# Opening of a vision transformer kernel by channel, the bias on TensorE, and the rounding of w1 in six halves

## What is computed

```python
y = einsum('bchw,rc->bhwr', x, W_repr) + b_repr        # 5 representations of 3 channels
h = patches of y (16 x 16) projected by W_proj (5, 192, 256), summed over the 5, + b_proj
h = h + attention(layernorm(h), W_qkv, W_out)          # 12 heads of 64, 36 tokens per image
z = layernorm(h)
expert = argmax(softmax(z @ gate_w + gate_b))          # 8 experts
h = h + (gelu(z @ w1[e] + b1[e]) @ w2[e] + b2[e])      # e is each token's expert
```

## Time and profile before

| | |
|---|---|
| time, median of 3 executions | 329.94 us (329.91 to 331.65) |
| the profiled execution's own time | 332.25 us |
| its span, first to last instruction | 330.5 us |
| mean granted clock of TensorE, share of full speed | 0.918 |
| busy: TensorE products | 280.2 us (85%) |
| busy: VectorE | 205.5 us (62%) |
| busy: ScalarE | 161.1 us (49%) |
| busy: GpSimd | 61.5 us (19%) |

### The profile page before, as it was taken

The page is one execution under the profiler, slowest core; times in us unless marked ns, Lnnn a source line. Parts: engine busy times, 40 slices in busy tenths (PEclk is TensorE's granted clock), DMA queues, the critical chain, the costliest instruction groups (busy, mean ns, idle before and its releaser), DMA issues.

```text
span 330.5 us, 6850 instructions
## 1 busy us (share of the span) xinstructions
PE 280.2 (85%) x2070; PEld 243.9 (74%) x2071; DVE 205.5 (62%) x585; ACT 161.1 (49%) x585; POOL 61.5 (19%) x105
## 2 busy tenths in 40 slices
PE   1677998899988899988899998957578999999982
PEld 1666887688967688967688876837467999988971
DVE  2986768835878836878825888144325565556530
ACT  3323488942579843578933479312014433442420
POOL 2711000103000103000103000020410443443231
PEclk9996999969999979999969999695959999999998
DMA  6889400000500000400000108756220122212100
GB/s 226 240 325 419 176 3 0 2 0 2 163 0 0 0 0 18 142 0 0 0 0 8 47 2 344 324 193 245 59 60 0 48 69 56 70 42 50 39 0 0
DMA packets 5727, 27.87 MB, mean 84 GB/s; under 512 B 1575, under 2 KB 2867, under 8 KB 5070
## 3 DMA queue, kind: packets, MB, share of 16 engines
q1 hardware_dynamic: 3630, 17.32, 15.0%
q10 hardware_dynamic: 288, 6.29, 4.6%
q0 software_dynamic: 1792, 4.04, 4.4%
HBM read 24.99 MB, written 3.34 MB: 86 GB/s over the span
## 4 chain that ended last, share of the span: by engine, by line
PE 61%; DVE 13%; ACT 11%; issue 8%; DMA 3%; POOL 1%; DVEq 1%; SPq 0%; POOLq 0%; ACTq 0%
PE psum L417 20%; PE psum L642 10%; PE psum L475 7%; ACT late L731 5%; PE psum L402 4%; PE psum L466 3%; PE psum L512 3%; PE psum L630 3%; PE psum L445 3%; PE psum L454 2%; DMA late<-w_proj 2%; DVE top L885 2%; DVE late L880 2%; DVE late L894 1%; DVE w1B L906 1%
## 5 line engine op out<-in xcount | busy, mean ns | idle before, releaser
L731 ACT ACTIVATE late<-late,top 108x108 f32<-108x108 f32 (+1 forms) x144 | 52.4, 373 | 3.3 <-DVE top L886 3.2
L417 PE MATMUL psum<-xn_hi,wq_parts 128*128 128x288 f32 x144 | 37.6, 329 | 2.4 <-DVE xnB_lo L862 1.4
L1186 POOL TENSOR_SCALAR veps<-mv 96x1 f32<-96x1 f32 x24 | 5.5, 229 | 180.9 <-DVE mv L844 180.5
L642 PE MATMUL psum<-w2s,kT 128*128 x192 | 34.7, 331 | 2.1 <-DVE kT L1113 1.3
L642 PEld LDWEIGHTS psum<-w2s,kT 128*128 128x128 f32 x192 | 30.8, 190 | 4.3 <-issue 4.2
L475 PE MATMUL psum<-wo,oT 128*96 128x192 f32 x144 | 31.0, 373 | 0.8 <-ACT oT L760 0.8
L417 PEld LDWEIGHTS psum<-xn_hi,wq_parts 128*128 128x128 f32 x144 | 25.9, 200 | 5.0 <-DVE rows L1004 1.7
L731 ACT ACTIVATION_READ_ACCUMULATOR late<-late,top 108x1 f32 (+1 forms) x144 | 28.4, 197 | 0.0
L475 PEld LDWEIGHTS psum<-wo,oT 128*96 128x96 f32 x144 | 26.1, 190 | 3.0 <-issue 1.4
L402 PE MATMUL psum<-late,xb 128*96 128x192 f32 x144 | 25.8, 331 | 2.9 <-issue 2.9
L454 PE MATMUL psum<-ident,late 108*108 108x108 f32 (+1 forms) x144 | 20.5, 270 | 8.7 <-DVE late L894 8.0
(11 more groups left out here) (157 smaller groups left out, 627.4 us busy)
## 6 DMA issues: line engine op xcount, KB each, us to landing
w2s<-w SPq DMA_DIRECT2D x1, 4608.0 KB, 15.0
xb<-xT SPq DMA_DIRECT2D x4, 864.0 KB, 6.9
w1A_in<-w ACTq DMA_DIRECT2D x1, 3072.0 KB, 10.2
w1B_in<-w ACTq DMA_DIRECT2D x1, 3072.0 KB, 18.7
late<-b SPq DMA_DIRECT2D x2, 1536.0 KB, 7.1
token_table<-rows SPq DMA_DIRECT2D x4, 432.0 KB, 3.4
late<-w_proj SPq DMA_DIRECT2D x1, 960.0 KB, 5.5
kT<-b SPq DMA_DIRECT2D x1, 768.0 KB, 11.4
```

Of the source, the lines that this page charges most:

```text
L417: mm = pe.matmul(dst, lhsT, rhs, start=(i == 0), stop=(i == len(parts) - 1))
L642: mm = pe.matmul(psum[:, 6, 0:D], hidT[i % 2][:, c * P:(c + 1) * P], w2s[:, bass.ds(e, 1), c, :], start=(c == 0), stop=(c == FCH - 1))
L731: ex = act.activation(head, head, ACT.Exp, bias=top[0:n, u % 3, i:i + 1], scale=LOGIT_SCALE, accum_out=total[0:n, u % 3, i:i + 1])
```

## The change

1. `w_repr` and `b_repr` come as one array, written out for 128 partitions by the host, in one load instead of two; `wr` and `br` are views of it.
2. The bias: `wb` and its five VectorE operations are gone. TensorE multiplies the projection itself with b_repr, a column of `br` repeated 96 times as the stationary operand, in ten products, and b_proj in an eleventh. ScalarE, not VectorE, copies the bias out of PSUM, between its two pairs of casts of w_qkv. The bias comes ahead of token tile 0.
3. The 32 transposes wait for the identity alone, not for w_proj.
4. `weff` is summed channel by channel with a semaphore for each. TensorE multiplies all three token tiles with channel 0, then channel 2 (GpSimd's), then channel 1, in three PSUM banks.
5. `split_wq` is parted in two. The second part for the first columns moves behind the three normalisations.
6. w1 is rounded in six casts of 1024 columns at steps 5 to 10 (for w1A two, for w1B's first half two, for its second two) instead of three of 2048 at steps 1, 3 and 5. VectorE's four subtractions stand at steps 6, 7 and 8 and behind the value copy (group 1, first half) at the seam, instead of steps 2, 3, 6 and 7.

```diff
-W1_ROUNDED, W1_SPLIT = [1, 3, 5], [2, 3, 6, 7]
+W1_HALF = W1_PIECE // 2
+W1_ROUNDED, W1_SPLIT = [5, 6, 7, 8, 9, 10], [6, 7, 8]
...
-OPENING = ([("tok", 0), ("bias",), ("tok", 1), ("tok", 2)] + [("xt", t) for t in range(NT)]
+OPENING = ([("bias",), ("tok", 0), ("tok", 1), ("tok", 2)] + [("xt", t) for t in range(NT)]
...
-            sp.dma_start(wr[:, :], w_repr.partition_broadcast(P)).then_inc(wp_here, 16)
+            sp.dma_start(wr_br[:, :], reps).then_inc(wp_here, 16)
...
-            sp.dma_start(br[:, :], b_repr.partition_broadcast(P)).then_inc(br_here, 16)
...
@@ TensorE
             pe.wait_ge(ident_ready, 1)
+            keep_clock(32)
+
             pe.wait_ge(wp_here, 32)
-            keep_clock(32)
-            pe.wait_ge(x_here, 16)
-            pe.wait_ge(weff_ready, 2)
-            tokens(0, product(("tok", 0), 0, opening=True))
-            pe.wait_ge(br_here, 32)
-            pe.wait_ge(wb_ready, 1)
             slot = product(("bias",), 0, opening=True)
             dst = into(slot)
-            pe.matmul(dst[0:TT, 0:D], ones[:, :], wb[:, 0, :], start=True, stop=False)
-            pe.matmul(dst[0:TT, 0:D], ones[:, :], wb[:, 1, :], start=False, stop=False)
+            for r in range(REPR):
+                for i in range(2):
+                    pe.matmul(dst[0:TT, 0:D], br[:, r:r + 1].to_broadcast([P, TT]), wp[:, i, r, :],
+                              start=(r == 0 and i == 0), stop=False)
+            pe.wait_ge(br_here, 16)
             pe.matmul(dst[0:TT, 0:D], ones[0:REPR, :], bp[:, :], start=False, stop=True).then_inc(full[slot[0]], 1)
-            for t in range(1, NT):
-                tokens(t, product(("tok", t), 0, opening=True))
+
+            pe.wait_ge(x_here, 16)
+            order = [0, 2, 1]
+            for c in order:
+                pe.wait_ge(weff_ready[c], 1)
+                for t in range(NT):
+                    slot = product(("tok", t), 0, opening=True)
+                    dst = into(slot) if c == order[0] else acc(slot[0])
+                    for i in range(2):
+                        mm = pe.matmul(dst[0:TT, 0:D], xb[:, 2 * c + i, t * TT:(t + 1) * TT], weff[:, c, i, :],
+                                       start=(c == order[0] and i == 0), stop=(c == order[-1] and i == 1))
...
@@ ScalarE
+                if i == 0:
+                    slot = product(("bias",), 0, opening=True)
+                    complete(act, slot)
+                    act.copy(bias[:, :], acc(slot[0])[0:TT, 0:D]).then_inc(free[slot[0]], 1)
...
-                cols = bass.ds(b * W1_PIECE, W1_PIECE)
-                if part == 0:
+                cols = bass.ds(b * W1_PIECE + (part % 2) * W1_HALF, W1_HALF)
+                if part < 2:
...
@@ VectorE, opening
-            for r in range(REPR):
-                for c in range(CHANNELS - 1):
+            for c in range(CHANNELS - 1):
+                for r in range(REPR):
...
-            dve.engine_nop().then_inc(weff_ready, 1)
-            dve.wait_ge(br_here, 32)
-            for r in range(REPR):
-                if r == 0:
-                    ins = dve.tensor_scalar(wb[:, :, :], wp[:, :, r, :], br[:, r:r + 1], None, ALU.mult)
...
-            split_wq(0)
-            slot = product(("bias",), 0, opening=True)
-            complete(dve, slot)
-            dve.tensor_copy(bias[:, :], acc(slot[0])[0:TT, 0:D]).then_inc(free[slot[0]], 1)
-            taken(dve, slot)
+                        if r < REPR - 1:
+                            own(ins)
+                        else:
+                            ins.then_inc(weff_ready[c], 1)
+            split_wqA(0)
+            taken(dve, product(("bias",), 0, opening=True))
             for t in range(NT):
                 take_tokens(t, product(("tok", t), 0, opening=True))
             for t in range(NT):
                 layernorm(xn[:, t, :], h[:, t, :], 0, t, t).then_inc(xn_ready, 1)
+            split_wqB(0)
             for t in range(NT):
                 take_xn_lo(t, product(("xt", t), 0, opening=True), t)
-            split_wq(1)
+            split_wqA(1)
+            split_wqB(1)
...
@@ VectorE, the seam, behind the value copies (0, 0), (0, 1), (1, 0)
                         take_v(g, f, product(("v", g, f), b))
                         if g == 0:
                             soften(f, b + 1)
+                    split_w1(b, 3)
```

More of the change, by code:

```diff
@@ L119, in product, with build @@
     return n % len(ACC), n // len(ACC) + blocks * (len(MIDDLE) // len(ACC))
-def build(nc, xT, w_proj, w_repr, b_repr, b_proj, w_qkv, w_out, gate_w, gate_b, w1, b1, w2, b2, out):
+def build(nc, xT, w_proj, reps, b_proj, w_qkv, w_out, gate_w, gate_b, w1, b1, w2, b2, out):
     table = nc.dram_tensor("token_table", [TOKENS + 1, 2 * D], F32, kind="Internal").ap()
@@ L295, in build @@
         consts_ready = sem("consts_ready")
-        weff_ready = sem("weff_ready")
+        weff_ready = [sem(f"weff_ready{c}") for c in range(CHANNELS)]
         scaled = sem("scaled")
-        wb_ready = sem("wb_ready")
         tiles_ready = sem("tiles_ready")
@@ L704, in round_w1 @@
             def round_w1(b, part):
-                cols = bass.ds(b * W1_PIECE, W1_PIECE)
-                if part == 0:
+                cols = bass.ds(b * W1_PIECE + (part % 2) * W1_HALF, W1_HALF)
+                if part < 2:
                     act.wait_ge(w1_here, 32)
                     act.copy(w1A_hi[:, cols], w1A_in[:, cols]).then_inc(w1A_hi_ready, 1)
-                elif part == 1:
+                elif part < 4:
                     act.wait_ge(w1_split, b + 1)
-                    act.copy(w1B_part[:, :], w1B_in[0:DB, cols]).then_inc(w1_hi_ready, 1)
+                    act.copy(w1B_part[:, (part % 2) * W1_HALF:(part % 2 + 1) * W1_HALF],
+                             w1B_in[0:DB, cols]).then_inc(w1_hi_ready, 1)
                 else:
@@ L863, in take_xn_lo, with split_wqA @@
                                   ALU.subtract).then_inc(free[slot[0]], 1)
-            def split_wq(i):
+            def split_wqA(i):
                 cols = WQ_PIECES[i]
@@ L897, in split_w1 @@
             def split_w1(b, i):
-                half, last_piece = W1_PIECE // 2, i == len(W1_SPLIT) - 1
-                cols = bass.ds(b * W1_PIECE + (i % 2) * half, half)
+                at = (i % 2) * W1_HALF
+                cols = bass.ds(b * W1_PIECE + at, W1_HALF)
                 if i < 2:
-                    dve.wait_ge(w1A_hi_ready, b + 1)
+                    dve.wait_ge(w1A_hi_ready, 2 * b + i + 1)
                     dve.tensor_tensor(w1A_lo[:, cols], w1A_in[:, cols], w1A_hi[:, cols], ALU.subtract)
                 else:
-                    dve.wait_ge(w1_hi_ready, b + 1)
-                    lo = dve.tensor_tensor(w1B[0:DB, cols], w1B_in[0:DB, cols],
-                                           w1B_part[:, (i % 2) * half:(i % 2 + 1) * half], ALU.subtract)
-                    if last_piece:
+                    dve.wait_ge(w1_hi_ready, 2 * b + i - 1)
+                    lo = dve.tensor_tensor(w1B[0:DB, cols], w1B_in[0:DB, cols], w1B_part[:, at:at + W1_HALF],
+                                           ALU.subtract)
+                    if i == 3:
                         lo.then_inc(w1_split, 1)
@@ L925, in _ @@
             dve.wait_ge(wp_here, 32)
-            for r in range(REPR):
-                for c in range(CHANNELS - 1):
+            for c in range(CHANNELS - 1):
+                for r in range(REPR):
                     s = r * CHANNELS + c
                     if r == 0:
-                        ins = dve.tensor_scalar(weff[:, c, :, :], wp[:, :, r, :], wr[:, s:s + 1], None, ALU.mult)
+                        own(dve.tensor_scalar(weff[:, c, :, :], wp[:, :, r, :], wr[:, s:s + 1], None, ALU.mult))
                     else:
@@ L1168, in _ @@
                 pool.wait_ge(scaled, r + 1)
-                own(pool.tensor_tensor(weff[:, CHANNELS - 1, :, :], wp_last[:, 0, :, :] if r == 1 else
-                                       weff[:, CHANNELS - 1, :, :], wp_last[:, r, :, :], ALU.add))
-            pool.engine_nop().then_inc(weff_ready, 1)
+                ins = pool.tensor_tensor(weff[:, CHANNELS - 1, :, :], wp_last[:, 0, :, :] if r == 1 else
+                                         weff[:, CHANNELS - 1, :, :], wp_last[:, r, :, :], ALU.add)
+                if r < REPR - 1:
+                    own(ins)
+                else:
+                    ins.then_inc(weff_ready[CHANNELS - 1], 1)
             pool.affine_select(out=before[:, :], in_=before[:, :], compare_op=ALU.is_gt, fill=0.0, base=0,
@@ L1261 @@
         "w_proj": np.asarray(L0_tok_W_proj).reshape(REPR, D, 2, P).transpose(3, 2, 0, 1),
-        "w_repr": np.asarray(L0_tok_W_repr).reshape(REPR * CHANNELS),
-        "b_repr": np.asarray(L0_tok_b_repr),
+        "reps": np.tile(np.r_[np.asarray(L0_tok_W_repr).reshape(-1), np.asarray(L0_tok_b_repr)], (P, 1)),
         "b_proj": np.asarray(L0_tok_b_proj),
```

17 lines of the change are left out of this document (7 added, 10 removed).

## The result

The changed kernel takes **319.82 us** (median of 4 executions, 319.42 to 320.78) against 329.93 us for the kernel before on the same chip (329.89 to 331.65). The ratio is 0.9686 with a 95% interval of [0.9648, 0.9724]: faster by 10.1 us, where 6.25 were forecast, and just past the fast end of the range (320.0). The profiled execution took 319.42 us for a span of 317.7; its mean granted clock is 0.94, and that of before was 0.918.

The account below looks back on a forecast made before the run. No single engine bounds the kernel everywhere (TensorE carries 61% of the chain); VectorE is the opening's path. Opening 4.1 plus blocks 2.15 gave 6.25 us off the 329.94 median: 323.7 us, range 320.0 to 328.6.

Parts of the forecast that it names:

- The opening: Start to first q and k products: bias sum leaves VectorE, first token tile at 16.95 us, products 4.1 us earlier.
- Channel 0's sum: Opening: first accumulation ends at 7.9 us, three more beside GpSimd's adds take about 1.3 each; ready at 11.8.
- The exclusive lock: Opening, rule against the forecast: VectorE waits out whole GpSimd adds, 1.81 us per later sum; gain 4.7 us, 325.2 us.
- rival E: Opening not freed, since the port rule or late bias products hold TensorE: 325.2 us; chance 0.04.
- Steps 1 to 4: Blocks 0 to 2: TensorE's 1.21 us wait for k's copy goes; block 0 gains 1.55 us, the others 1.8 by step 4.
- No slack, no wait: Steps 5 to 7: ScalarE delivers the first half rounding at 59.9 us, just when VectorE asks, at no cost.
- rival B: Steps 5 to 7: VectorE waits for half roundings, blocks give nothing, seams cost 1.0 three times: 328.8 us; chance 0.14.
- The seam: Between two blocks: the fourth subtraction, 1.21 us, delays everything by 1.0 us; TensorE's wait of 1.01 becomes 2.0.
- the blocks: All blocks together: 1.55 + 0.8 + 0.8 - 1.0 = 2.15 us gained.
- The sum: Whole kernel: opening 4.1 plus blocks 2.15 gives 6.25 us, median 323.7 us; chance 0.62.
- C: Seams: 2.0 us idle drops TensorE's clock, 3.4 us each, 10.2 at three seams: 333.9 us, slower; chance 0.08.
- D: Behind unit 7: shorter waits keep the clock high, 1.2 us won in each of three blocks: 320.1 us; chance 0.12.

Follow-up runs that it names:

- the filled kernels: The kernel before and the changed kernel, each with 70 more transposes that only keep TensorE busy behind the last block: 326.29 us and 318.09 us.
- the run with the seam relieved: The changed kernel with VectorE's fourth subtraction of w1 moved from between values and gate logits to behind the low parts of xn: 318.56 us.
- the rounding alone: The kernel before with only the six half roundings of w1 and the four moved subtractions: 325.5 us.
- the filled opening: The changed kernel with 18 idle transposes ahead of the opening's transposes of xn and 16 behind them: 318.19 us.
- the late subtractions with the tail filled: The changed kernel with all four subtractions of w1 behind step 8, roundings at steps 3, 4, 7 to 10, and the tail's idle transposes: 313.07 us.
- the one with 0.95: The changed kernel with late subtractions and the tail's idle transposes: 313.07 us; with the opening's idle transposes as well 310.11 us.
- the replicated array alone: The kernel before with w_repr and b_repr in one replicated array and nothing else: 330.46 us against 330.12.

## Where the prediction was right, and the step that failed

**The opening: right, 0.6 us too small.** Foreseen were transposes from 1.8 us, the bias done by 12.2, VectorE at tile 0 at 16.95, products at 24.1. Measured: 1.81, 11.6, 16.41 and 23.48. TensorE decided tile 0, by 0.29 us. Its chain had errors both ways. The transposes took 6.03 us, not 5.35: the first 22 started 0.21 us apart and the others 0.11, where in the kernel before only the first 16 were slow. The eleven bias products then took 3.9 us, at the fast end of the 4.0 to 5.0 foreseen, and the eighteen token products 6.09, not 6.5. VectorE's start at 6.30 instead of 6.82 gives 0.2 us of the rest at most, since with a start at 6.82 it would have been ready at 16.65.

Channel 0's sum was ready at 10.6 us instead of 11.8. The term had three accumulations of 1.3 us beside GpSimd's additions; two were beside them, at 1.24 and 1.23 us. It was not waited for, since the bias ended later.

The exclusive lock of the Trainium skill (SBUF — State Buffer, "Who interferes with whom") is not refuted by that, as the prediction had it. It took the rule to mean a whole addition of 1.19 us waited for each time, 1.81 us each and the channel ready at 13.4. That did not happen, and rival E with it. But each accumulation that began during an addition ended 0.4 us behind it, here and in the kernel before (four of 1.23 to 1.37 us). This is what one would see if VectorE waited for the rest of the addition that runs, and no longer.

**Steps 1 to 4: right to a few hundredths.** 1.55, 1.8 and 1.8 us foreseen, 1.56, 1.81 and 1.83 measured (at the normalisation of step 5).

**"No slack, no wait": wrong in size.** I had ScalarE deliver the half rounding just when VectorE asks and took that as free. It came 0.19 us late, the steps 5 to 7 cost 0.28 us in each of three blocks, and TensorE, which had shed small waits ahead, waited 2.00 us before unit 7 instead of the 1.2 foreseen. This is a sliver of rival B. A cover without any slack should have had a price in the sum.

**The seam: right in kind, 0.3 us too dear.** I carried the whole subtraction less 0.15 us of idle time through to TensorE (1.0 us, wait 2.0). It was 0.7 us and 1.3: with VectorE later, the small gaps behind the logits shrank (6.53 to 6.34 us) and those ahead did too. The prediction read this stretch as one without a gap; there are several, and the earlier trace rows shows one of 0.58 us. Undone, it gave back just that in the trace.

So the blocks came to 2.26 us where 2.15 stood, by two errors that cancel (-0.84, +0.9), and all waits to 7.0 where 6.25 stood.

**The sum: the step that failed.** It added waits and took the granted clock as it was, with "1.7 us either way" for every start of a slow stretch and nothing in the middle. The result lies 3.9 us beyond its 6.25: 0.7 us are waits, and 3.1 us are clock, a term that the sum put at nothing. By the medians of the filled kernels some 1.9 of the 3.1 lie in the tail, a part of the kernel that the change does not touch and that I did not look at, and 1.2 in the opening and the blocks. Between the two profiled executions the clock's share is larger, 5.8 us: 1.1 because the slow stretch of the opening now lies over waiting time (it begins 3.2 us ahead of the q products instead of 0.8), 1.8 in the blocks and 2.9 in the tail. My rows on the clock end at 94 us; the page's own clock line shows the two slow stretches behind 220 us. With that line in the argument the sum would still not have been certain, since how the tail would fall against its slow stretches could not be read from before, but the range would have reached some 3 us further on the fast side. What stays open is why the tail of the change keeps its clock behind 222 us where the same instructions lose it at 239 us in before; the run with the seam relieved loses it too.

**The rivals.** B happened in small. C's mechanism happened twice, behind one seam each of the rounding alone and of the filled opening, and in none of the change's trace. D's 320.1 us is the number next to the measured 319.82, but by luck: the clock stayed low behind unit 7 in all three blocks of the change, and what it gained lay mostly elsewhere. D is real all the same: where the wait there is 0.95 us, two of the three stretches vanish in one trace, and all three in that of the late subtractions with the tail filled. The Trainium skill (TensorE: Matmul & The Clock Gate, "HAM oscillation — how this bites in real kernels") warns of waits between bursts. Its own case has waits of 3 to 5 us for DMAs; here the clock fell at unit 7 with waits of 0.95 to 2.00 us, so it can fall behind shorter ones too. In the tail, filling the waits of the kernel before left one slow stretch of 3.4 us of two of 10.2, at a gain of 3.9 us (330.2 to 326.29).

## What to carry to other kernels

Read the clock line of the whole page before adding up waits: a kernel whose clock falls in stretches gets a second term, of either sign, in places that the change does not touch, and the range must hold it. TensorE can be kept busy with idle products where it waits, but the gain need not last: in the traces the same fillers were worth nothing by the end of block 2 on the kernel with waits of 2.00 us, and 1.8 us up to the last block on the one with 0.95. By the medians they gave 1.6 us (across two sessions) and 3.0 us. That the shorter waits are the reason is likely, not shown. Work that needs no data belongs in the time before the first load lands; with the new arithmetic in place, that exchange of two lines decided over more than 4 of the opening's 4.7 us.

## What the runs showed that was not expected

Two profiled executions of the same program can differ by 1.4 us in the blocks with every wait equal, by the length of slow stretches alone. Over the executions of the kernel before, time and mean granted clock move together: 323.07 us at 0.956, 327.32 at 0.938, 330.2 at 0.933, 332.18 at 0.923, 333.18 at 0.917. The gain of this change is as large as that span, so medians over several executions were needed.

The load of w_proj lands about 0.5 us earlier in every kernel with the new opening (VectorE begins at 6.3 us; 5.0 us from issue to landing against 5.5), but only 0.1 us earlier with the replicated array alone (6.71), and as early (6.28) where TensorE stands idle while it runs. So it is neither the array alone nor TensorE's activity; what it is stays open.
